# Products without a reader in TensorE's waits, and two key products moved ahead of the second mixture's last second layers

## The chip, the core and the metric

The kernel runs on one core of one Trainium2 chip. The metric is the device time of one execution in microseconds (us); a kernel's time is the median of several executions. TensorE multiplies matrices into PSUM, VectorE (DVE) and ScalarE (ACT) read PSUM and write PSUM or SBUF, GpSimd (POOL) works on SBUF, and SyncE issues the DMAs. The engines run side by side and wait for each other through semaphores. Each engine executes its own instructions in the order in which they are written. TensorE's clock has two levels in the trace, 2.4 GHz (shown as 1.00) and 1.2 GHz (0.50).

## The reference, cut to what matters

Input is x of 8 batches of 128 rows with 128 columns, and a context of the same shape. Four layers follow each other, each made of an attention-like part and a feed-forward part, and both add to x:

```python
x = x + tanh(g_xattn[0]) * mlstm(layernorm(x), ctx, ctx, ...)             # recurrence
x = x + tanh(g_ffn[0])   * pick_one_of_8(layernorm(x), ...)               # first mixture
x = x + tanh(g_xattn[1]) * attention_16_heads(layernorm(x), ctx, ctx)     # first attention
x = x + tanh(g_ffn[1])   * ternary_linear(layernorm(x))                   # rows scaled to 8 bits
x = x + tanh(g_xattn[2]) * attention_mask_group(layernorm(x), ctx, ctx)   # second attention
x = x + tanh(g_ffn[2])   * top_8_of_64_experts(layernorm(x))              # second mixture
x = x + tanh(g_xattn[3]) * attention_relative_bias(layernorm(x), ctx)     # third attention
x = x + tanh(g_ffn[3])   * (shared + top_2_of_8)(layernorm(x))            # third mixture
```

An attention is `softmax(q k^T / sqrt(8) + bias) v` per head, then an output projection. An expert is `silu(x Wg) * (x Wu)` times a weight of its token, then `Wd`.

## The kernel before, in words

The whole of x stays in SBUF. A product of 32-bit precision is made of three 16-bit products, high by high, high by low, low by high (`three` and `products`, L235 and L225), so that one product over half of the tokens is three instructions of 512 columns. Nearly every product is issued at L228.

The three attentions are numbered a = 0, 1, 2. Each has three stretches:

- The head (`head_pe`, `head_act`, `head_dve`): normalisation, the turn of the normalised x by TensorE (L460), and 16 jobs e = 0 to 15 (keys and queries, `proj_pe`), each three products by TensorE, one activation by ScalarE (L1782) and one sum by DVE (L1789). Jobs 0 and 1 of a head are keys, need only the context, and are issued earlier: for a = 2 in `turn_y_pe`, after the second mixture's last second layer and ahead of the turn of its result (L1653).
- The attention itself (`att_pe`): per batch b, scores by rows (`att_rows`, L1893), their maxima by DVE (L1915), the maxima turned (`att_max_pe`; L1950 and L1952 for a = 0, L1948 for the others), scores by columns (`att_cols`, L1984), the exponentials by ScalarE (L2002), their products with the values (`att_pv`, L2021 and L2027), the quotient by DVE (L2035), the output product (`att_out`, L228). For a = 1 there are six small DVE instructions after the maxima (`att_max_split`, L1925 to L1934) and a multiplication by POOL (L2006). The last jobs 13, 14 and 15 of the head stand among the first scores.
- The tail, inside `att_pe`, after the last batch's scores: the last two output products, the residual by DVE (L2072), the normalisation of the last three batches, and their turn (`turn_one_pe`, L481), ScalarE's high part (L485), DVE's low part (L489). For a = 1 and 2 the router of the next mixture follows (`route_pe`, 24 small products; `route_dve`, L936 to L974).

The mixtures run over chunks of 128 hidden units: 48 for the second (`moe1_pe`), 10 for the third (`moe_pe`). Per chunk TensorE makes a gate product, an up product and a second layer (`moe_pe_down`) for each half of the tokens. In the second mixture DVE multiplies gate by up (L1115, raises `w1_gated`), weighs (L1128) and takes the low part (L1264); ScalarE makes SiLU (L1064) and the high part (L1093). At the end ScalarE copies the two halves of the result (L1675), TensorE turns them (L1653), and DVE adds them to x (L1698). The first instructions of the third head's DVE program are these sums.

`fill_pe(pe, at, n)` (L784) issues n products of 128 x 128 by 512 columns of the context into bank `at`; nobody reads the result. The kernel before uses it in the recurrence and in the first mixture only (58 products in all). PSUM has 8 banks of 512 columns; which one a product writes decides whom it must wait for.

## Time and profile before

| | |
|---|---|
| median of 3 runs | 635.67 us (635.35 to 637.15) |
| the profiled execution's own time | 636.67 us |
| its span, first to last instruction | 634.9 us |
| mean granted clock of TensorE | 0.962 |
| busy: TensorE, DVE, ACT, POOL | 562.7, 518.2, 340.1, 249.3 us |
| `fill_pe` products (L787) | 58, 16.5 us busy |

The profiled execution took 1.8 us more than its span. Its mean clock is below 1 because the granted clock goes to 0.50 in eight stretches, 47.8 us in all. The first, at 45.45 to 48.86 us, is at the end of the recurrence. By time the span is: recurrence to about 49 us, first mixture to 120, first attention with its head and tail to 190, second to 284, second mixture to 501, third attention to 582, third mixture to the end.

### The profile page before, as it was taken

To read this page: it belongs to the slowest core of one execution; us is meant where nothing else is said; L and a number is where in the kernel's file an instruction comes from. 1 tells how busy PE (TensorE), PEld (TensorE's weight loads), DVE (VectorE), ACT (ScalarE), POOL (GpSimd) and SP (SyncE) were. 2 spreads that over 40 slices of the span, in tenths; PEclk is the share of its full clock that TensorE was granted. 3 is DMA by queue.
4 is the path that set the end of the run, shared out by engine and by line. 5 is a ranking of instruction groups with operands and counts; after the bars stand their busy time and mean duration, and the time that the engine had idled before them with its cause. 6 is when DMAs were issued, how large, how long until landed. Compare 5 with 4: busy or idle time off the path is not lost.

```text
span 634.9 us, 16313 instructions
## 1 busy us (share of the span) xinstructions
PE 562.7 (89%) x5394; PEld 289.0 (46%) x5394; DVE 518.2 (82%) x1136; ACT 340.1 (54%) x675; POOL 249.3 (39%) x456
## 2 busy tenths in 40 slices
PE   4899899968878799967999999999999779996997
PEld 2444588725644255533444343333433325553443
DVE  6798886877889778848899999999999786766896
ACT  3878776555545333434555565555655463343654
POOL 3475010301772168872344443444334100234452
PEclk9999999987998799979999999999999899997999
DMA  8600200240000000002566656666666000001110
GB/s 316 214 2 2 69 3 2 40 117 2 4 2 0 2 2 3 3 1 69 155 179 176 175 170 162 180 181 169 163 173 182 4 2 2 2 3 31 38 50 33
DMA packets 34912, 48.89 MB, mean 77 GB/s; under 512 B 6756, under 2 KB 26800, under 8 KB 34472
## 3 DMA queue, kind: packets, MB, share of 16 engines
q1 hardware_dynamic: 34424, 47.40, 26.4%
q8 instruction: 37, 0.61, 0.4%
q10 hardware_dynamic: 432, 0.73, 0.3%
q14 instruction: 19, 0.16, 0.1%
HBM read 47.29 MB, written 0.82 MB: 76 GB/s over the span
## 4 chain that ended last, share of the span: by engine, by line
PE 44%; DVE 41%; ACT 6%; issue 4%; POOL 3%; DMA 1%; DVEq 0%; ACTq 0%; POOLq 0%
PE PS L228 29%; DVE PS L1115 9%; DVE SHARED L1264 5%; DVE SHARED L1789 4%; DVE PS L1128 3%; PE PS L2021 2%; ACT SHARED L1093 2%; PE PS L2027 2%; DVE MB L1915 2%; ACT SHARED L1064 2%; PE PS L1893 2%; DVE REC L2035 1%; DVE PS L1915 1%; DVE STAT L394 1%; DVE XN L410 1%
## 5 line engine op out<-in xcount | busy, mean ns | idle before, releaser
L1093 ACT ACTIVATE SHARED<-PS 128x512 f16<-128x512 f32 x96 | 57.1, 597 | 71.8 <-DVE PS L1128 68.2
L228 PE MATMUL PS<-XH,UH 128*128 128x512 f16 x232 | 89.9, 387 | 6.2 <-DVE PS L1115 3.4
L228 PE MATMUL PS<-XL,UH 128*128 128x512 f16 x232 | 89.5, 386 | 0.0
L228 PE MATMUL PS<-XH,UL 128*128 128x512 f16 x232 | 89.4, 385 | 0.0
L2002 ACT ACTIVATE SHARED<-PS 128x512 f32<-128x512 f32 x96 | 52.2, 595 | 64.9 <-PE PS L228 49.7
L228 PE MATMUL PS<-SHARED,DNH 128*128 128x512 f16 x232 | 69.9, 383 | 4.6 <-DVE SHARED L1264 3.7
L1264 DVE TENSOR_TENSOR SHARED<-PS,SHARED 128x512 f16<-128x512 f32 x96 | 62.0, 686 | 6.8 <-ACT SHARED L1093 3.4
L1064 ACT ACTIVATE SHARED<-PS 128x512 f32<-128x512 f32 x96 | 57.2, 597 | 17.4 <-PE PS L228 15.0
L1022 POOL CAST DNH<-DF 128x128 f16<-128x128 f32 x58 | 19.0, 327 | 117.2 <-DMA DF<-in_down 100.7
L1128 DVE TENSOR_TENSOR PS<-PS,SHARED 128x512 f32<-128x512 f32 x92 | 59.7, 694 | 3.8
L1115 DVE TENSOR_TENSOR PS<-SHARED,PS 128x1024 f32<-128x1024 f32 x46 | 56.5, 1229 | 6.7 <-PE PS L228 0.7
L1915 DVE TENSOR_REDUCE MB<-PS 128x4 f16<-128x512 f32 x64 | 41.1, 687 | 16.8 <-PE PS L228 11.0
L2006 POOL TENSOR_TENSOR SHARED<-SHARED,GPT 128x512 f32<-128x512 f32 x32 | 40.0, 1270 | 26.2 <-ACT SHARED L2002 26.1
L1782 ACT ACTIVATE SHARED<-PS,LOB,LOM 128x512 f16<-128x512 f32 x48 | 35.2, 774 | 25.8 <-PE PS L228 25.8
L228 PEld LDWEIGHTS PS<-XH,UH 128*128 128x128 f16 x232 | 22.9, 99 | 50.5 <-DVE PS L1115 25.1
L228 PE MATMUL PS<-SHARED,DNL 128*128 128x512 f16 x116 | 44.5, 384 | 0.0
L1015 POOL TENSOR_TENSOR UL<-UF,UH 128x256 f16<-128x256 f32 x58 | 39.2, 676 | 4.6
L2021 PE MATMUL PS<-SHARED,ONE 128*32 128x128 f32 x768 | 40.7, 285 | 0.0
L2027 PE MATMUL PS<-SHARED,V 128*32 128x128 f32 x768 | 39.4, 278 | 0.6 <-POOL SHARED L2006 0.6
L1789 DVE SCALAR_TENSOR_TENSOR SHARED<-PS,BQK,SHARED 128x512 f16<-128x512 f32 x48 | 33.5, 738 | 6.9 <-ACT SHARED L1782 6.8
L228 PEld LDWEIGHTS PS<-SHARED,DNH 128*128 128x128 f16 x232 | 22.3, 98 | 33.9 <-issue 7.3
L228 PEld LDWEIGHTS PS<-XH,UL 128*128 128x128 f16 x232 | 23.0, 99 | 28.4 <-issue 1.7
(345 smaller groups left out, 1275.5 us busy)
## 6 DMA issues: line engine op xcount, KB each, us to landing
SHARED<-w_rows_dram SPq DMA_DIRECT2D x31, 384.0 KB, 3.6
SHARED<-w_rows_dram SPq DMA_DIRECT2D x30, 256.0 KB, 3.8
UF<-in_up SPq DMA_DIRECT2D x58, 128.0 KB, 3.4
SHARED<-w_rows_dram SPq DMA_DIRECT2D x31, 128.0 KB, 2.7
DF<-in_down SPq DMA_DIRECT2D x58, 64.0 KB, 3.0
V<-in_up SPq DMA_DIRECT2D x2, 1024.0 KB, 9.1
SHARED<-in_down SPq DMA_DIRECT2D x4, 512.0 KB
SHARED<-t_values_dram SPq DMA_DIRECT2D x2, 1024.0 KB, 10.5
```

Source lines behind the costliest of these rows:

```text
L228: last = pe.matmul(dst, l, r, start=start and i == 0, stop=stop and i == len(pairs) - 1)
L1064: act.activation(SG1[u][:, hf, :], bank(hf), ACT.Silu).then_inc(sem("e_act"), 1)
L1093: act.activation(HHI[:, u, hf, :], bank(4 + hf) if m == 1 else HF[:, hf, :], ACT.Copy).then_inc(sem("e_high"), 1)
L1115: dve.tensor_tensor(dst, SG1[u].rearrange("p i n -> p (i n)"), bank(2, 2), ALU.mult).then_inc(sem("w1_gated"), 1)
L1128: dve.tensor_tensor(bank(4 + hf), bank(4 + hf), WB[u][:, HALF * hf:HALF * hf + HALF], ALU.mult)\
L1264: dve.tensor_tensor(HLO[:, u, hf, :], src, HHI[:, u, hf, :], ALU.subtract).then_inc(sem("e_low"), 1)
L1789: dve.scalar_tensor_tensor(dst, proj_bank(a, "kq", e), BQK[:, a, "qk".index(c), g:g + 1], TLO[:, e % 4, :], ALU.add, ALU.subtract).then_in ...
L1915: dve.tensor_reduce(dst, src, AX, ALU.max, negate=True).then_inc(sem("a_max"), 1)
L2002: act.activation(PF[:, j, :], bank(2 + j % 2), ACT.Exp).then_inc(sem("a_exp"), 1)
L2006: pool.tensor_tensor(PG[:, j, :].rearrange("p (g s) -> p g s", g=4), PF[:, j, :].rearrange("p (g s) -> p g s", g=4), over(GPT[:, b, :], 4) ...
L2021: pe.matmul(bank(4 + u)[32 * g:32 * g + 32, 128:256], ONE8[:, j, :], PF[:, j, 128 * g:128 * g + 128], start=j == 0, stop=j == 3, skip_grou ...
L2027: last = pe.matmul(bank(4 + u)[32 * g:32 * g + 32, 0:128], V32[:, b, 4 * g + j, :], src[:, j, 128 * g:128 * g + 128], start=False, stop=j ...
```

## The change

It adds calls of `fill_pe` on TensorE's queue at places of the attentions: around the first batch of the first two attentions (`FILL`, 16 and 13 products), in the second head ahead of and behind the first turn (7 and 2), in the tails of the second and the third attention (`FILL_TAIL` and a last 2: 22 and 18), and at the end of the second mixture (3). These are 81 products. Each group stands directly ahead of an instruction with a wait. It also moves jobs 0 and 1 of the third head: on TensorE from behind the last second layers to ahead of them, with a wait on `w1_gated` for DVE's product of the last chunk, because these jobs write banks 2 and 3, from which that product reads; on ScalarE from behind the two copies of the mixture's result to ahead of them. Since `turn_y_pe` is reached for m = 1 and 2 only, the lines taken out of it were executed for m = 1 alone. No computed value changes.

```diff
--- before.py
+++ after.py
@@ -1241,6 +1241,10 @@
                 step(2 * i + 1, 1, i)
             step(CH2 - 2, 0, CH2 // 2 - 1)
             step(CH2 - 1, 1, CH2 // 2 - 1)
+            pe.wait_ge(sem("w1_gated"), CH2)
+            for e in (0, 1):
+                proj_pe(pe, 2, "k", e)
+            fill_pe(pe, 0, 3)
             for hf in range(2):
                 moe_pe_down(pe, 1, CH2 - 1, 1, hf, stop=True)
             turn_y_pe(pe, 1)
@@ -1644,9 +1648,6 @@
 
         def turn_y_pe(pe, m):
 
-            if m < 2:
-                for e in (0, 1):
-                    proj_pe(pe, 2 * m, "k", e)
             for i in range(2):
                 pe.wait_ge(sem("y_out"), 2 * m - 1 + i)
                 for b in range(4 * i, 4 * i + 4):
@@ -1668,6 +1669,8 @@
                     moe_act_high(act, m, c, u, hf)
             if m == 1:
                 moe1_act(act)
+                for e in (0, 1):
+                    proj_act(act, 2, "k", e)
             else:
                 chunks(act, m, step)
             for i in range(2):
@@ -1802,8 +1805,11 @@
             proj_pe(pe, a, "v", 0)
             if a != 1:
                 proj_pe(pe, a, "v", 1)
+            if a == 1:
+                fill_pe(pe, 0, 7)
             turn_pe(pe, TURN[a], NORM[a], (0,), TURN_AT)
             if a == 1:
+                fill_pe(pe, 5, 2)
                 quant_turn_pe(pe, 1)
                 proj_pe(pe, a, "k", 4)
                 quant_product_pe(pe, 1)
@@ -1821,7 +1827,7 @@
                 proj_pe(pe, a, "kq"[e >= 8], e)
 
         def head_act(act, a):
-            for e in range(4):
+            for e in range(2 if a == 2 else 0, 4):
                 proj_act(act, a, "k", e)
             proj_act(act, a, "v", 0)
             if a != 1:
@@ -2075,6 +2081,9 @@
 
         NEXT = ((3, None), (5, 4), (7, 6))
 
+        FILL = ((6, 0, 3, 3, 4), (2, 7, 0, 0, 4), (0, 0, 0, 0, 0))
+        FILL_TAIL = (None, (2, 6, 3, 2, 7), (3, 2, 3, 2, 6))
+
         def att_pe(pe, a):
             k, j = NEXT[a]
             if a == 2:
@@ -2082,8 +2091,10 @@
                 pe.wait_ge(sem("ld_late"), 16 * len(LATE))
             att_rows(pe, a, 0, 0)
             proj_pe(pe, a, "q", 13)
+            fill_pe(pe, 4, FILL[a][0])
             att_rows(pe, a, 0, 1)
             proj_pe(pe, a, "q", 14)
+            fill_pe(pe, 4, FILL[a][1])
             att_max_pe(pe, a, 0, 0)
             proj_pe(pe, a, "q", 15)
             att_rows(pe, a, 1, 0)
@@ -2092,13 +2103,19 @@
                 u = b % 2
                 if b == 1:
                     pe.wait_ge(sem("p_lo"), 16 * (a + 1))
+                if b == 0:
+                    fill_pe(pe, 4, FILL[a][2])
                 att_cols(pe, a, b, u, 0)
+                if b == 0:
+                    fill_pe(pe, 4, FILL[a][3])
                 if b + 1 < NB:
                     att_rows(pe, a, b + 1, 1)
                 if b >= 1:
                     att_pv(pe, a, b - 1, 1 - u, 2)
                     att_pv(pe, a, b - 1, 1 - u, 3)
                 att_cols(pe, a, b, u, 1)
+                if b == 0:
+                    fill_pe(pe, 4, FILL[a][4])
                 if b + 1 < NB:
                     att_max_pe(pe, a, b + 1, 1 - u)
                 if b >= 2:
@@ -2116,15 +2133,22 @@
             if a == 0:
                 quant_product_pe(pe, 0)
                 proj_pe(pe, 1, "k", 0)
+            if j:
+                fill_pe(pe, 2, FILL_TAIL[a][0])
             att_out(pe, a, NB - 2, 0)
             if a == 0:
                 proj_pe(pe, 1, "k", 1)
             if j:
+                fill_pe(pe, 2, FILL_TAIL[a][1])
                 turn_one_pe(pe, a, j, k, NB - 3)
+                fill_pe(pe, 2, FILL_TAIL[a][2])
             att_out(pe, a, NB - 1, 1)
             if j:
+                fill_pe(pe, 2, FILL_TAIL[a][3])
                 turn_one_pe(pe, a, j, k, NB - 2)
+                fill_pe(pe, 2, FILL_TAIL[a][4])
                 turn_one_pe(pe, a, j, k, NB - 1)
+                fill_pe(pe, 2, 2)
 
         def att_act(act, a):
             k, j = NEXT[a]
```

## Rows read from the trace of the kernel before

**Rows 1.** The page: TensorE's clock in 40 slices, the chain's shares by engine.
```profile
PEclk9999999987998799979999999999999899997999
...
PE 44%; DVE 41%; ACT 6%; issue 4%; POOL 3%; DMA 1%; DVEq 0%; ACTq 0%; POOLq 0%
```

**Rows 2.** Stretches (from:to, length; busy PE, PEld, DVE, ACT, POOL; clock; DMA).
```profile
137.61:141.02 3.41, 3.24 (x11) 1.01 (x9) 2.06 (x4) 0.78 (x1) 0.00 (x0) 0.50 0.00 0
144.43:151.26 6.83, 5.80 (x99) 4.10 (x97) 3.86 (x6) 2.77 (x5) 0.00 (x0) 0.50 0.01 2
195.63:199.05 3.42, 2.75 (x14) 1.55 (x14) 3.38 (x8) 1.97 (x3) 0.00 (x0) 0.50 0.00 0
212.70:219.53 6.83, 5.83 (x33) 2.11 (x35) 3.81 (x9) 1.42 (x3) 0.16 (x1) 0.50 0.02 5
277.55:287.79 10.24, 6.06 (x39) 3.10 (x40) 4.36 (x19) 1.97 (x6) 6.41 (x14) 0.50 0.07 19
496.01:499.42 3.41, 3.02 (x8) 1.12 (x9) 0.83 (x2) 0.98 (x3) 0.00 (x0) 0.50 0.00 0
577.92:588.16 10.24, 7.05 (x41) 2.88 (x41) 6.71 (x44) 3.33 (x7) 4.84 (x12) 0.50 0.17 46
```

**Rows 3.** TensorE in order of time, start of the second attention.
```profile
211.49 0.38 PE L228 MATMUL PS<-XH,WRL 128*128 128x512 f16 x1
213.70 0.61 PE L1948 MATMUL PS<-EYEH,MB 128*128 128x128 f16 x4 [1.83 <-DVE MB L1934]
214.10 0.63 PE L228 MATMUL PS<-XH,WRH 128*128 128x512 f16 x1
214.53 0.64 PE L228 MATMUL PS<-XL,WRH 128*128 128x512 f16 x1
...
222.85 0.40 PE L1948 MATMUL PS<-EYEH,MB 128*128 128x128 f16 x4 [1.19 <-DVE MB L1934]
```

**Rows 4.** TensorE and DVE in order of time, start of the first attention.
```profile
137.13 0.40 PE L1893 MATMUL PS<-SHARED 24*128 24x128 f16 x8 [1.78 <-DVE MB L1915]
...
147.47 1.30 DVE L1915 TENSOR_REDUCE MB<-PS 128x4 f16<-128x512 f32 x2 [1.66 <-PE PS L1893]
...
151.64 0.96 DVE L2035 RECIPROCAL REC<-PS 128x128 f32<-128x128 f32 x1 [0.35 <-PE PS L2027]
```

**Rows 5.** The second head: a wait of TensorE, and a stretch as in rows 2.
```profile
194.55 1.09 PE L460 MATMUL PS<-EYE,XN 128*128 128x128 f32 x4 [2.05 <-DVE XN L410]
...
193.00:206.00 13.00, 10.78 (x60) 5.46 (x60) 12.96 (x37) 7.23 (x12) 2.10 (x3) 0.87 0.00 0
```

**Rows 6.** The chain that ended last (start, us, what), second attention's tail and router.
```profile
279.12 0.84 PE PS L228 x5
...
282.78 0.49 PE PS L481
...
283.95 1.48 PE PS L228 x24
```

**Rows 7.** In order of time: the end of the second mixture.
```profile
492.93 1.23 DVE L1115 TENSOR_TENSOR PS<-SHARED,PS 128x1024 f32<-128x1024 f32 x1
...
494.93 1.19 ACT L1093 ACTIVATE SHARED<-PS 128x512 f16<-128x512 f32 x2 [2.85 <-DVE PS L1128]
...
496.40 1.01 PE L228 MATMUL PS<-SHARED,DNH 128*128 128x512 f16 x2 [2.59 <-DVE SHARED L1264]
...
500.01 1.45 ACT L1782 ACTIVATE SHARED<-PS,LOB,LOM 128x512 f16<-128x512 f32 x2 [0.26 <-PE PS L228]
...
501.10 0.75 DVE L1698 SCALAR_TENSOR_TENSOR X<-PS,G,X 128x512 f32<-128x512 f32 x1 [4.25 <-PE PS L1653]
```

**Rows 8.** In order of time, then a stretch: third attention's tail, third mixture.
```profile
581.34 0.47 PE L481 MATMUL PS<-EYE,XN 128*128 128x128 f32 x1 [1.39 <-DVE XN L410]
...
588.08 0.22 DVE L974 TENSOR_TENSOR CW<-SHARED,CW 128x64 f16<-128x64 f32 x1
...
589.00:625.00 36.00, 36.00 (x168) 16.23 (x167) 32.36 (x50) 21.25 (x36) 19.90 (x31) 1.00 0.15 39
```

## The prediction

> **What bounds the kernel now.** I read the slices of the page first. TensorE's clock is full in most of them and lower in eight or nine, and the chain that ended last is shared almost evenly by TensorE and DVE [rows 1]. So no engine bounds the whole; each stage has to be read by itself. Then I read the stretches of low clock [rows 2]: seven, at half clock throughout, 3.41 us or two or three times that long, 44.4 us together. All lie where this change works: the start of the first attention (two), the second head, the start of the second attention, the second attention's tail, the end of the second mixture, the third attention's tail. Last I read TensorE in order of time ahead of each. It had waited for DVE shortly before: 1.78 us at 137.13 [rows 4], 2.05 us at 194.55 [rows 5]; the 1.83 us ahead of 213.70 [rows 3] and the 2.59 us ahead of 496.40 [rows 7] lie across the fall itself. The cause of a fall is thus little work for TensorE, and its price is paid by whatever TensorE does next. A low stretch costs something only where TensorE, not DVE, is late in it.
>
> **The price of a product.** At full clock 168 products, nearly all of 512 columns, fill 36.00 us [rows 8], 0.22 us each; at low clock two such start 0.43 us apart (214.10 and 214.53) [rows 3]. A reader-less product therefore costs 0.22 us of TensorE's queue, and nothing of the time if it fits the wait behind it. The groups against their waits: 6 products, 1.3 us, before the wait of 1.78 [rows 4]; 7, 1.5 us, before 2.05 [rows 5]; 7, 1.5 us, before 1.83, and 4, 0.9 us, before 1.19 [rows 3]; 3, 0.7 us, before 2.59, with the two key jobs (six products, 1.3 us) ahead of them [rows 7]; 6, 1.3 us, before 1.39 [rows 8]. Each fits at full clock, the last one barely, so I cost the 81 products at nothing. If none were hidden they would cost 81 x 0.22 = 17.8 us; that is the bound on the other side. They read the context and write a bank that is free at that place, and no other engine waits for them.
>
> **First attention's start: 3.0 us gained.** With 1.3 us of products in the wait before 137.13, and 10 more in the waits of the first batch, the clock has no reason to fall at 137.61 or at 144.43. What was slow between 137.61 and 151.26 was partly TensorE: DVE was busy only 2.06 of 3.41 and 3.86 of 6.83 us there [rows 2]. I follow the chain. Jobs 14 and 15 and the turned maxima end 1.1 us earlier (nine products of 512 columns or their like, half of it behind DVE). The second batch's scores and the first batch's eight groups of value products, then at half price, end 1.9 us earlier; DVE's waits such as the 1.66 us before 147.47 go. The first reciprocal, at 151.64 [rows 4], comes at about 148.6. Behind it DVE sets the pace and the shift stays.
>
> **Second head: nothing.** DVE was busy 12.96 of the 13.00 us around the low stretch [rows 5]. TensorE's slower products there were covered by DVE. Its clock rises, the time does not.
>
> **Second attention's start: 2.0 us.** Between 212.70 and 219.53 TensorE was busy 5.83 of 6.83 us and DVE 3.81 [rows 2]. Job 15, sixteen small products and nine of 512 columns stand between 213.70 and 219.4. At full clock they need about 3 us instead of 5.7. Some 0.7 us of this go to DVE's own work (job 15's sum and the maxima follow each other), so the turn at 222.85 [rows 3] comes about 2.0 us earlier.
>
> **Second attention's tail and router: 1.2 us.** The chain runs through TensorE four times: turns of 0.49 us twice (the second at 282.78), an output product of 0.84, 24 router products of 1.48 [rows 6]. At full clock I take 0.14 off each turn, 0.28 off the output product and 0.6 off the router (24 x 0.025). The rest of the tail is a relay of ACT, DVE and POOL, whose steps no clock changes. The 22 products lie in its gaps. Bounds: 0 if the clock falls all the same, 1.3.
>
> **End of the second mixture: 2.2 us.** Here the order is what counts. TensorE stood for 2.59 us before the last second layers (496.40), which wait for DVE's low parts, then made these six products and the two key jobs at low clock, and only then the turns that DVE's sum at 501.10 waits for [rows 7]. After the change the key jobs run in the wait. They need `w1_gated` of the last chunk, DVE's product at 492.93, which ends at 494.2 [rows 7]; with three fillers they end at 496.1, ahead of the second layers' own release, just under 496.4. Behind this new wait stand only instructions that waited anyway. ScalarE now makes the two key activations (1.45 us, before at 500.01) ahead of the copies of the result; it is free for them from 496.1, when the last high parts end [rows 7], so the copies, which I take at 0.6 us, start at about 497.6. The turns no longer stand behind the key jobs, the first half is copied at 498.2 and turned at 498.8, and DVE's sum comes at 498.9 instead of 501.10. DVE sets the pace of the head that follows, so 2.2 us stay; 1.5 of them would come from order alone with the clock up in both kernels. POOL and SyncE have no step in this; the queues' DMAs are unchanged.
>
> **Third attention's tail and router: 0.3 us.** Two turns and an output product, 0.3 us at full clock. The rest of the low stretch, the third mixture's first twelve products (5.2 us at low clock, 2.6 at full), stands beside the router's DVE chain, which ends at 588.08 [rows 8] and on which TensorE's next turn waits. So these 2.6 us are not gained.
>
> **What it may trigger.** They come back as an idle stretch instead. At full clock TensorE ends the twelve products at about 585.5 and waits until 587.8, 2.3 us or more, as long as the waits ahead of the falls above. I expect a fall there; it would reach into the third mixture, where TensorE is busy 36.00 of 36.00 us [rows 8]. The shortest stretch of rows 2, 3.41 us, then costs half of itself, 1.7 us. The same can happen in the second mixture's first 10 us, where the router's chain is DVE's too; half of such a stretch would meet TensorE's own path.
>
> **The sum.** Against the profiled execution, 636.67: less 3.0 + 2.0 + 1.2 + 2.2 + 0.3 = 8.7, plus 1.7 for one new low stretch in a mixture, gives 629.7. The median of the three runs is 1.0 us below the profiled one. I don't take this off: the runs differ by where their low stretches lie, I suppose, and the change removes most of these.
>
> The Trainium skill ("TensorE: Matmul & The Clock Gate", section "What's actually happening") says that the penalty of the slow ramp is below 1% of a typical kernel's span and that the count of slow products differs from run to run. That speaks against a gain above 6.3 us: by it the time would be 630.3 or more. Here the trace has 44.4 us at half clock in the places named, 7% of the span [rows 2], so I go by the rows; the forecast needs nothing of the page.
>
> **Rivals.** (a) As summed, one new fall: 629.7, chance 0.45. (b) No new fall: the idle stretch before 587.8 is short enough, or its place relative to the clock's decision is lucky: 628.0, chance 0.30. For it: there are waits of more than 1 us that no fall follows, such as the one before 222.85 [rows 3]. (c) New falls in both mixtures, each 1.7: 631.4, chance 0.12. For it: both routers are the same kind of DVE chain. (d) The products don't hold the clock, the low stretches stay, and only the moved key jobs pay: 636.67 - 2.2 = 634.5, chance 0.08. Against it: the stretches in front of the falls are nearly idle, and the change fills half or more of each. (e) Slower: the clock is already low when TensorE reaches the fillers. Then each costs 0.43 us, and the waits are too short. The three groups of 6, 7 and 7 at the starts and the head would be late by 0.8, 1.0 and 1.2 us and the 6 of the last tail by 1.2, together 4.2 us for 26 products; 81 at that rate give 13, less 2.2 for the order: 647. It decides from the point where a group is longer than its wait: at low clock 4 products fill 1.78 us. Chance 0.05. Against it: rows 3 show full clock up to 211.49, directly ahead of a group.
>
> **How the numbers follow.** The likeliest case is (a). From 0.2 under (b)'s time less the 1.0 us of the unprofiled runs, to (c) plus 1.2, the range is 626.8 to 632.6; outside lie (d), (e) and tails of (b) and (c), about 2 in 10. A difference of 0.3%, 1.9 us, is about what a measurement of this kernel can tell from no change. Faster by more than that: (a), (b), (c), 0.87. Within: (d), 0.08. Slower: (e), 0.05.
>
> **What would show it.** In the changed kernel's trace the clock should be 1.00 from 130 to 200 us and again in the second attention's start; the reciprocal that was at 151.64 should be at about 148.6, the turn at 222.85 about 5.0 earlier, the router of the second mixture 6.2 earlier, the sum at 501.10 8.4 earlier, and a low stretch should appear at the third mixture's beginning. The waits of TensorE in front of which fillers stand should have shrunk, not vanished; one that is gone, with DVE or ACT waiting behind it, is a filler that delays. The prediction is wrong if the second head gains, if the shift of one attention's start is lost before its tail (then POOL, not DVE, sets the pace there), or if low stretches stay where the fillers are.

## The result, and the profile after

| | before | after |
|---|---|---|
| median, from lowest to highest (20 executions each, on the same chip) | 637.44 us (633.83 to 640.27) | 634.79 us (630.25 to 637.13) |
| profiled execution | 636.67 us | 634.09 us |
| its span | 634.9 us | 632.3 us |
| mean granted clock of TensorE | 0.962 | 0.989 |
| low clock within the span | 47.8 us in eight stretches | 13.7 us in three stretches |

The ratio of after to before is 0.995, with a 95% interval of 0.9932 to 0.9968: faster, by 2.65 us where 7.0 were forecast against the profiled execution. 629.7 was predicted, with a range of 626.8 to 632.6, and 634.79 lies outside it.

One part of the gap between the medians is in no profile. The 20 executions of the changed kernel took 1.7 to 1.8 us more than their spans. Those of the kernel before, in the runs made beside the experiments, took 1.7 to 3.1 us more, with medians of 2.1 to 2.8. No run here settles why.

The page of the changed kernel, where [rows 1] stood before: the slices of TensorE's clock and the shares of the chain that ended last.

```profile
PEclk9999999999999999997999999999999899999999
DVE 43%; PE 40%; ACT 7%; issue 4%; POOL 3%; DMA 1%; DVEq 0%; ACTq 0%; POOLq 0%
```

The clock is held nearly everywhere now. Next, the changed kernel by stretches, with the busy time and count of TensorE, its weight loads, DVE, ACT and POOL, then the granted clock, the DMA share and GB/s. The first two lines cover the starts of both attentions; the other five are the three low stretches and what stands directly ahead of two of them.

```profile
130.00:200.00 70.00, 58.87 (x983) 34.68 (x984) 60.49 (x139) 38.02 (x71) 31.61 (x56) 1.00 0.07 18
205.00:280.00 75.00, 70.10 (x1012) 36.63 (x1012) 54.55 (x150) 28.13 (x60) 50.84 (x61) 1.00 0.01 2
284.10:290.93 6.83, 3.44 (x16) 1.79 (x17) 4.96 (x9) 3.65 (x7) 1.32 (x3) 1.00 0.01 2
290.93:297.76 6.83, 6.83 (x15) 1.97 (x13) 3.90 (x5) 1.79 (x3) 1.06 (x2) 0.50 0.73 199
502.55:505.97 3.42, 3.42 (x12) 1.71 (x11) 3.42 (x9) 2.15 (x3) 0.00 (x0) 0.50 0.01 2
581.06:584.47 3.41, 0.43 (x7) 0.34 (x7) 3.10 (x11) 1.36 (x3) 1.07 (x2) 1.00 0.23 67
584.47:587.89 3.42, 3.42 (x14) 1.44 (x11) 2.19 (x5) 2.55 (x4) 0.00 (x0) 0.50 0.00 0
```

The seven stretches of [rows 2] are gone, and the one at the recurrence's end with them. Three new ones are there: 290.93 to 297.76 in the second mixture's first chunks, 502.55 to 505.97 in the third head, and 584.47 to 587.89 in the third mixture. In the first and the third TensorE is busy all the time and DVE is not (3.90 of 6.83, 2.19 of 3.42 us): there TensorE is late, and the low clock costs time. In the second DVE is busy 3.42 of 3.42 us, and it costs nothing: in the table below the changed kernel gains 0.2 us from 501.10 to 583.35, as routers_filled does, which has no such stretch.

**Where the time went.** DVE executes the same instructions in both kernels, so each can be paired with itself. A shift is its start in one kernel less its start in the profile of before, in us. These are pairs of single profiled executions, good for saying where time moved; how much a kernel gains is read from its ratio. The other kernels are those of the next section.

| DVE instruction, place (start before) | after | routers_filled | tails_empty | order_alone | tails_alone |
|---|---|---|---|---|---|
| first reciprocal, first attention (151.64) | -2.68 | -1.98 | -2.73 | +0.25 | -0.41 |
| last job of the second head (207.10) | -2.66 | -1.96 | -2.17 | +0.27 | +0.66 |
| last small instruction of the maxima, second attention (222.57) | -4.48 | -3.79 | -4.00 | -1.56 | -1.10 |
| reciprocal ahead of its tail (275.69) | -4.44 | -3.75 | -3.98 | -1.53 | -1.07 |
| second router's first (285.45) | -5.58 | -4.89 | -3.98 | -1.70 | -2.21 |
| weighing in the second mixture's first chunk (296.82) | -5.50 | -4.89 | -3.66 | -1.17 | -1.26 |
| the same in its next chunk (301.43) | -2.25 | -4.89 | -3.66 | +1.75 | +1.12 |
| last gated product (492.93) | -2.18 | -4.88 | -3.62 | +1.87 | +1.19 |
| first sum into x (501.10) | -4.58 | -7.28 | -6.02 | -0.52 | +1.40 |
| third router's first (583.35) | -4.77 | -7.47 | -6.02 | -0.32 | +1.22 |
| third router's last (588.08) | -4.23 | -6.93 | -5.38 | -0.30 | +1.76 |
| SiLU product in the third mixture (600.15) | -2.57 | -6.93 | -5.38 | -0.29 | +3.42 |

Rows of the changed kernel from which seven of the first column's entries come: start, duration, engine, line, operation. The lines of the changed kernel that are quoted here stand up to six lower than in the kernel before (L2041 is L2035 there).

```profile
148.97 0.95 DVE L2041 RECIPROCAL REC<-PS 128x128 f32<-128x128 f32 x1
279.87 0.69 DVE L936 COPY SHARED<-PS 128x512 f32<-128x512 f32 x1 [0.97 <-PE PS L228]
291.32 0.70 DVE L1123 TENSOR_TENSOR PS<-SHARED,PS 128x512 f32<-128x512 f32 x1 [2.02 <-PE PS L1212]
299.18 0.70 DVE L1123 TENSOR_TENSOR PS<-SHARED,PS 128x512 f32<-128x512 f32 x1 [2.27 <-PE PS L1212]
...
496.52 0.75 DVE L1701 SCALAR_TENSOR_TENSOR X<-PS,G,X 128x512 f32<-128x512 f32 x1 [1.85 <-PE PS L1654]
...
583.85 0.23 DVE L974 TENSOR_TENSOR CW<-SHARED,CW 128x64 f16<-128x64 f32 x1
...
597.58 0.69 DVE L1102 TENSOR_TENSOR SHARED<-SHARED,PS 128x512 f32<-128x512 f32 x1
```

So the change gains 2.7 + 1.8 + 1.1 + 2.4 + 0.2 = 8.2 us in five places and gives 5.5 back in three: 3.3 between 296.82 and 301.43, 0.5 inside the third router, 1.7 behind it. That leaves 2.7, against the 2.6 between the two profiled executions.

**Two of the five gains are not shown to be the products'.** They are measured against one execution that was at low clock at 212.70 and at 496.01 [rows 2]. order_alone and tails_alone have no product at the second attention's start, and gain 1.8 us there all the same (+0.27 to -1.56, +0.66 to -1.10), because their executions did not fall there. starts_alone (shifts -2.93 at 492.93 and -4.41 at 501.10) has the old order and no product at the end of the second mixture, and gains 1.5 us there at full clock. The first line is order_alone's, the second starts_alone's:

```profile
212.70:219.53 6.83, 4.86 (x50) 2.10 (x51) 4.87 (x13) 2.11 (x4) 2.01 (x2) 1.00 0.02 5
489.00:499.00 10.00, 6.99 (x46) 3.95 (x47) 6.96 (x17) 5.20 (x9) 0.56 (x2) 1.00 0.03 9
```

The other two larger gains do hang on the products. At the first attention's start the two kernels without them are within 0.4 us of before (+0.25, -0.41). In the second attention's tail, from 275.69 to 285.45, tails_alone gains 1.1 us as the changed kernel does, and tails_empty nothing.

**Why the clock falls at the second mixture's start.** TensorE of the changed kernel in order of time, the idle time before an instruction in brackets.

```profile
285.15 0.38 PE L228 MATMUL PS<-XH,UH 128*128 128x512 f16 x1 [2.27 <-ACT SHARED L1064]
...
288.23 1.06 PE L1255 MATMUL PS<-EYE,SHARED 128*64 128x128 f32 x8 [1.62 <-DVE SHARED L953]
...
290.01 2.91 PE L1212 MATMUL PS<-SHARED,SELF 64*128 64x512 f32 x4 [0.72 <-ACT SHARED L1262]
...
293.26 0.63 PE L228 MATMUL PS<-XL,UH 128*128 128x512 f16 x1
```

Three waits, 2.27 + 1.62 + 0.72 = 4.6 us, stand close together ahead of the fall at 290.93. The first is for ScalarE's SiLU, the second for the router's DVE chain. The kernel before has the same three, of 1.49, 1.62 and 0.72 us, and its profiled execution did not fall there, so the change made only the first longer, by 0.8 us. The third mixture's start has one long wait for the router's chain, 2.98 us. The kernel before had none there, because TensorE at low clock was busy until the chain had ended. First two rows of the changed kernel, then one of before:

```profile
584.13 0.76 PE L902 MATMUL PS<-EYEH,CW 128*128 128x128 f16 x8 [2.98 <-DVE CW L974]
584.69 0.63 PE L228 MATMUL PS<-XH,UH 128*128 128x512 f16 x1
```

```profile
588.37 0.62 PE L902 MATMUL PS<-EYEH,CW 128*128 128x128 f16 x8
```

### The profile page after: what moved, and what is told of

It is laid out like the page before. It is cut to its first block, busy times and chain, and to the rows that moved or that the text cites. A ratio compares the mean times of both kernels' runs of the same rounds, so it can differ in the third digit from the quotient of the medians.

```text
span 632.3 us, 16475 instructions
## 1 busy us (share of the span) xinstructions
PE 572.3 (91%) x5475; PEld 291.5 (46%) x5475; DVE 519.3 (82%) x1136; ACT 340.0 (54%) x675; POOL 248.7 (39%) x456
## 4 chain that ended last, share of the span: by engine, by line
DVE 43%; PE 40%; ACT 7%; issue 4%; POOL 3%; DMA 1%; DVEq 0%; ACTq 0%; POOLq 0%
PE PS L228 28%; DVE PS L1115 9%; DVE SHARED L1268 5%; DVE SHARED L1792 4%; DVE PS L1128 3%; ACT SHARED L1093 2%; DVE MB L1921 2%; PE PS L2027 2%; ACT SHARED L1064 2%; PE PS L1899 2%; PE PS L2033 2%; DVE PS L1921 2%; DVE STAT L394 1%; DVE XN L410 1%; DVE REC L2041 1%
## 5 line engine op out<-in xcount | busy, mean ns | idle before, releaser
L1785 ACT ACTIVATE SHARED<-PS,LOB,LOM 128x512 f16<-128x512 f32 x48 | 35.3, 774 | 23.3 <-PE PS L228 23.3
L1015 POOL TENSOR_TENSOR UL<-UF,UH 128x256 f16<-128x256 f32 x58 | 38.8, 669 | 4.6
L787 PE MATMUL PS<-CHI 128*128 128x512 f16 x139 | 36.4, 380 | 0.0
```

## The experiments

Twelve kernels ran, in three groups; the kernels of one group share a chip and the runs of the kernel before. Only fill_between, the last, has runs of its own of the kernel before. Each ratio is against these runs. Their medians lie between 636.29 and 638.74 us, so across groups ratios are compared, and within a group the kernels' own times as well.

**First group: the change taken apart, and its repair.**

The repair, routers_filled, is the changed kernel with 29 more reader-less products in the waits of both routers:

```diff
                 moe1_pe_up(pe, c, u)
+                if static and c == 0:
+                    fill_pe(pe, 4, 9)
...
                 if static and c == 0:
+                    fill_pe(pe, 4, 6)
                     moe1_rows_pe(pe)
+                    fill_pe(pe, 6, 2)
...
                 if isinstance(c, int) and c == 0:
+                    fill_pe(pe, 4, 12)
                     route_turn_pe(pe, 2)
```

> The changed kernel plus 29 reader-less products in TensorE's waits beside the routers: 9 and 6 of them around the second chunk's gate product of the second mixture, 2 ahead of its first weights' products, 12 ahead of the turn of the third mixture's router. Theory 1, the gain is given back by new falls of the clock at the starts of both mixtures: the low stretches at 291 to 298 us and at 584 to 588 us go, 3.3 and 1.3 to 1.7 us come back, and the median is about 5 us below the changed kernel's 634.8, near 630 (ratio to the kernel before 0.988). Theory 2, the shift is lost at the mixtures for another reason (weights that arrive when they arrive, DVE): the median stays at 634.8 or rises with the added products, and the shift against the kernel before shrinks at 293 to 301 us as it did.

Measured: 629.87 us (628.86 to 630.34), ratio 0.9863 [0.9828, 0.9899]. Its profile, by stretch, then its TensorE at the two routers:

```profile
190.00:600.00 410.00, 388.03 (x3164) 178.87 (x3164) 342.65 (x659) 205.79 (x364) 167.71 (x313) 1.00 0.33 87
```

```profile
283.41 2.11 PE L787 MATMUL PS<-CHI 128*128 128x512 f16 x9
...
285.84 0.38 PE L228 MATMUL PS<-XH,UH 128*128 128x512 f16 x1 [0.33 <-ACT SHARED L1064]
...
578.29 2.75 PE L787 MATMUL PS<-CHI 128*128 128x512 f16 x12
581.43 0.62 PE L902 MATMUL PS<-EYEH,CW 128*128 128x128 f16 x8 [0.39 <-DVE CW L974]
581.89 0.38 PE L228 MATMUL PS<-XH,UH 128*128 128x512 f16 x1
```

The clock is full from 190 to 600 us; two low stretches are left ahead of that, at 124.52 and 179.13. The wait of 2.27 us has become nine products and 0.33, the wait of 2.98 has become twelve and 0.39; neither router is later for it. The table of shifts shows both losses gone: 3.3 us at the second mixture's start and 1.7 behind the third router are exactly what the two low stretches had cost. The 0.5 us inside the third router stays.

order_alone is the kernel before with the two key jobs moved, on TensorE as below and on ScalarE as in the change, and no product added:

```diff
+            pe.wait_ge(sem("w1_gated"), CH2)
+            for e in (0, 1):
+                proj_pe(pe, 2, "k", e)
             for hf in range(2):
                 moe_pe_down(pe, 1, CH2 - 1, 1, hf, stop=True)
```

> The kernel before with the two key jobs of the third head moved ahead of the second mixture's last second layers, on TensorE and ScalarE, and no added reader-less product. If order is what pays there, as predicted: 1.5 us from order alone where the clock is up, 2.2 us with it, so DVE's first sum of the third head comes 1.5 to 2.2 us earlier against its neighbours and the median is about 2 us below the kernel before (ratio 0.997). Rival: the order only pays together with the clock that the three products hold up; then 0 to 0.7 us.

Measured: 635.87 us (634.12 to 636.98), ratio 0.996 [0.9935, 0.9986]. From 492.93 to 501.10 its shift goes from +1.87 to -0.52, a gain of 2.4 us. The changed kernel gains the same 2.4 there, so its three products at that place add nothing. Of the 2.4, 1.5 come to starts_alone by the clock alone, in the old order; the new order itself is worth the 0.9 that are left, by the difference of two single pairs. In the profile a low stretch at the second mixture's start hides all of it, which this execution had and the profiled one of before had not:

```profile
294.58:301.40 6.82, 6.82 (x14) 2.08 (x13) 3.90 (x5) 1.27 (x3) 1.07 (x2) 0.50 0.74 196
```

It costs 3.4 us (-1.70 at 285.45 to +1.75 at 301.43) in a kernel in which that place is as it was before. So this fall is not the products' alone: the kernel before can meet it too, and its profiled execution had been spared it.

tails_empty is the changed kernel without the 40 products of the two tails:

```diff
-        FILL_TAIL = (None, (2, 6, 3, 2, 7), (3, 2, 3, 2, 6))
+        FILL_TAIL = (None, (0, 0, 0, 0, 0), (0, 0, 0, 0, 0))
...
-                fill_pe(pe, 2, 2)
```

> The changed kernel without the 40 reader-less products in the tails of the second and the third attention. Theory 1, a low stretch in a tail is cheap because the routers' DVE chain covers the products behind it, and holding the clock there only moves the fall into the mixtures: the tails run at low clock as before (1.1 and 0.3 us lost), the mixtures start at full clock (3.3 and 1.7 us gained back), and the median is 2 to 3.6 us below the changed kernel's 634.8, near 632. Theory 2, the tails' products pay as intended: the median is 1.4 us above the changed kernel's, near 636.

Measured: 631.33 us (630.97 to 632.38), ratio 0.9891 [0.9855, 0.9926]. It is faster than the whole change, with more low clock. The interval lies apart from the change's [0.9932, 0.9968]; it overlaps a little with that of changed_again below, whose 12 executions have a median of 633.79 us. Its stretches:

```profile
272.77:283.01 10.24, 5.25 (x37) 2.84 (x38) 4.37 (x19) 2.51 (x7) 6.41 (x14) 0.50 0.08 19
291.00:298.00 7.00, 6.27 (x22) 2.43 (x20) 4.35 (x7) 3.27 (x6) 1.06 (x2) 1.00 0.49 135
573.14:579.97 6.83, 4.40 (x33) 2.04 (x34) 4.16 (x33) 1.89 (x4) 4.12 (x10) 0.50 0.21 60
```

17 us at half clock in the tails cost 1.1 + 0.2 us, because TensorE is busy about half of them and the relay of ACT, DVE and POOL sets the pace. But with the tails at low clock both mixtures start at full clock. Guarding a cheap place had moved the fall to a dear one. Of the four profiles in which neither the tails nor the second router are guarded (before, order_alone, tails_empty, starts_alone) one fell at the second mixture's start; of the five with the tails guarded and that router not, all did.

starts_alone is the kernel before with the 29 products at the two attentions' starts (`FILL` as in the change, nothing else).

> The kernel before with the 29 reader-less products at the starts of the first two attentions alone. By the predicted sum 3.0 + 2.0 us are gained there (in the changed kernel's profile 2.7 and 1.0 to 1.6 were), the tails run at low clock as before, and nothing else moves: the median is 4 to 5 us below the kernel before (ratio 0.993). Rival: with the starts at full clock other stretches fall in their place, in the second head for one, and the ratio is above 0.997.

Measured: 632.9 us (632.04 to 633.24), ratio 0.9911 [0.9875, 0.9946]. Its shift is -2.16 at the first reciprocal, -3.07 at 222.57, and stays near -3 to 492.93. A low stretch in the second head, 192.23 to 199.06, costs 0.9 of that (shift -2.16 to -1.31). These 29 products alone do at least as well as the whole change (the intervals overlap by little). Of its -3.8 us at the end of the profile, two terms, 1.8 and 1.5 us, are those that are not shown to be the products' (above).

**Second group: single parts, and the tails.**

head_empty is the changed kernel without `fill_pe(pe, 0, 7)` and `fill_pe(pe, 5, 2)` in the second head.

> The changed kernel without the 7 and 2 reader-less products in the second head. DVE covers TensorE there, so a low stretch in the head costs 0 to 0.3 us: DVE's instructions behind the head keep their shift against the kernel before, about -2.7 us up to 213 us, and the median is that of the changed kernel, 634.8, within the noise. Rival: the head's products pay, and the shift at 213 us shrinks by 1 us or more.

Measured: 635.57 us (630.48 to 636.98), ratio 0.9942 [0.9911, 0.9974], not to be told from the change by the median. In the profile a low stretch came back; its line among the stretches, then one row of DVE:

```profile
192.23:199.06 6.83, 6.31 (x23) 2.97 (x24) 6.80 (x23) 2.97 (x5) 0.23 (x1) 0.50 0.00 0
```

```profile
203.09 1.42 DVE L1792 SCALAR_TENSOR_TENSOR SHARED<-PS,BQK,SHARED 128x512 f16<-128x512 f32 x2 [0.82 <-ACT SHARED L1785]
```

DVE is busy 6.80 of 6.83 us in it, as in [rows 5], and yet the shift goes from -2.74 to -1.42. Some 0.35 of that is lost ahead of the head, at a low stretch of this execution in the first attention's tail (178.58 to 181.99). The rest, 1.0, comes in one step: the jobs that TensorE and ACT made late are missed by DVE only after the stretch, at 203.09. The nine products are worth 1.0 us in this profile, where the stretch is twice as long as the one of before.

third_router is the changed kernel with the 12 products ahead of the third router's turn, and nothing at the second.

> The changed kernel plus the 12 reader-less products ahead of the turn of the third mixture's router, and none in the second mixture. If each new fall has its own price: no low stretch at 584 us, the shift at the end of the span keeps what it had at 583 us (1.3 to 1.7 us more than in the changed kernel), the second mixture's start still loses up to 3.3 us in most executions; the median is near 633.3. Rival: the gain of the two fillings together came from the second mixture alone; then the median stays at 634.8.

Measured: 634.53 us (630.19 to 634.98), ratio 0.9933 [0.9904, 0.9963]. The third mixture starts at full clock and keeps its shift, -2.20 from 588.08 to the end. The gain is not seen in the time, because the second mixture fell for longer:

```profile
285.92:299.58 13.66, 12.28 (x29) 4.52 (x27) 7.48 (x12) 4.11 (x7) 1.07 (x2) 0.50 0.42 118
```

That stretch cost 4.9 us (shift -5.20 at 285.45, -0.31 at 301.43). The same place cost 3.3 to 3.4 in every profile with a stretch of 6.8 us there (after, changed_again, head_empty, tails_alone, order_alone), half of its length. What an unguarded wait costs goes by the length of the stretch, and that differs between executions of nearly the same kernel.

routers_no_tails is routers_filled without the tails' 40 products (the edit of tails_empty).

> The changed kernel with the 29 products beside the routers and without the 40 in the tails. Theory 1: with the mixtures' starts guarded the tails' products keep what they gain there, 1.2 + 0.3 us, so this kernel is about 1.5 us slower than the one with both, 631.4 against 629.9. Theory 2: the tails' products gain nothing even then, and this kernel is equal or faster, 629.9 or less.

Measured: 631.91 us (631.81 to 633.35), ratio 0.9898 [0.9861, 0.9935]. Against routers_filled in profile it is 0.8 us behind after the second tail (-4.09 against -4.89 at 285.45), 1.2 at 501.10, 1.5 at 588.08 and 2.2 at 600.15 (-4.76 against -6.93). The last 0.7 are not the tails' own. With the tails at low clock TensorE reaches the 12 products of the third router later, and they end behind the router's chain (the turn L902 waits for nothing):

```profile
581.02 2.75 PE L787 MATMUL PS<-CHI 128*128 128x512 f16 x12
583.61 0.61 PE L902 MATMUL PS<-EYEH,CW 128*128 128x128 f16 x8
```

So the same 40 products that make the changed kernel slower (0.995 with them, 0.9891 without, the intervals apart) are worth about 2 us once the routers are guarded. And the routers' 29 without the tails' 40 bring nothing over tails_empty (631.91 against 631.33 us). They pay only together.

tails_doubled is routers_filled with every group of the tails at twice its size (`FILL_TAIL` (4, 12, 6, 4, 14) and (6, 4, 6, 4, 12), and 4 for the last 2).

> The kernel with the 29 products beside the routers, and every group in the two tails doubled (4, 12, 6, 4, 14, 4 and 6, 4, 6, 4, 12, 4 products). The groups are then longer than their waits, by 0.2 to 1.3 us each at 0.22 us a product: about 2.5 us late in the second attention's tail, about 2.9 us in the third's, so 5 us above the 629.9 of the kernel with single groups, near 635. If the waits absorb them or the engines behind cover them, it stays under 632; a price of 0.22 us for all 40 added products would give 638.7.

Measured: 633.9 us (633.35 to 634.92), ratio 0.9931 [0.9904, 0.9959]. In profile it is 4.1 us behind routers_filled, with a mean clock of 0.997. Up to the second tail it was 0.75 us ahead (-4.50 against -3.75 at 275.69), so the doubling costs 4.8: 3.0 in the second tail, 1.5 in the third, 0.4 between them. Twelve products fill 2.75 us, so the 40 more are 40 x 0.22 = 8.8 us, of which 4.8 came through and the rest still fitted the waits. The forecast of 5 had the right size: a group that outgrows its wait delays at once, at full clock too.

**Third group: repeated, turned around, and extended.**

changed_again is the changed kernel once more.

> The changed kernel itself, on the chip of the two others, to tell how far its profile varies. By theory 1 its executions differ by which stretches fall: the shift against the kernel before is -8 us less what the falls at the mixtures' starts take, 0 to 5.5 us, and the executions with the higher mean clock are the faster ones, at about 1 us for a low stretch of 3.41 us (0.0027 of mean clock). Median near 634.8.

Measured: 633.79 us (630.49 to 635.56), ratio 0.9932 [0.9904, 0.996]. The same two falls are in its profile, in other places by 0.4 us:

```profile
291.30:298.13 6.83, 6.83 (x15) 1.89 (x13) 3.90 (x5) 1.79 (x3) 1.06 (x2) 0.50 0.79 212
584.85:588.26 3.41, 3.41 (x12) 1.22 (x9) 2.27 (x5) 2.55 (x4) 0.00 (x0) 0.50 0.00 0
```

Over its 12 executions and the 20 of the first measurement, time and granted clock go together (correlation -0.89). The three shortest of the 20, 630.25 to 630.62, have clocks of 0.992 to 0.997; the five longest, 636.17 to 637.13, have 0.978 to 0.981. The mean clock is not all: at 0.992 changed_again has executions of 630.6 and of 634.37 us, the second of them the profiled one with both falls in the mixtures. Where the low stretches lie counts too.

tails_alone is the kernel before with the tails' 40 products alone.

> The kernel before with the 40 reader-less products in the tails alone. Theory 1: 1.1 and 0.3 us are gained in the tails, and new low stretches at the starts of the second and the third mixture take up to 3.3 and 1.7 us, so the kernel is 0 to 3 us slower than the kernel before (ratio 1.000 to 1.005). Theory 2, the tails pay by themselves: 1.4 us faster (ratio 0.998).

Measured: 639.91 us (633.16 to 641.02), ratio 1.0015 [0.998, 1.005]. The two stretches in the profile, which stood in neither mixture before:

```profile
293.40:300.23 6.83, 6.83 (x12) 2.35 (x13) 2.97 (x5) 1.19 (x2) 0.19 (x1) 0.50 0.62 172
590.36:593.78 3.42, 3.42 (x15) 1.50 (x13) 2.10 (x4) 2.54 (x4) 0.00 (x0) 0.50 0.00 0
```

They cost 3.3 us (-2.21 at 285.45 to +1.12) and 1.7 (+1.76 to +3.42). The median lies 3.6 us above that of before in this group, while the ratio's interval has 1 in it. Half of the change by count of its products brings no measurable gain and moves the low clock from the tails, where it costs 1.3, into the mixtures, where it costs 5.0 in this profile. The 12 executions lie in two clusters, five at 633.2 to 635.3 and seven at 639.7 to 641.0 us; the profiled one, 640.12, is of the upper. That the lower five were spared the falls is likely, but no trace of one shows it.

fuller is routers_filled with 17 more products in the remaining waits of the third attention's start and of the two ends of the first attention.

> The kernel with the 29 products beside the routers and 17 more: 2 and 4 in the first attention's tail, 5 ahead of the third attention's first scores, 6 in its first batch. In the profile of the kernel without these a low stretch at 179 to 182.5 us took about 1 us. If the products hold the clock there as elsewhere and are hidden, the median is about 1 us lower, 629, and the executions lie closer together; if they are late at the tail's short waits (0.9 and 0.5 us), it is 0.2 to 1 us higher.

Measured: 629.35 us (629.08 to 630.13), ratio 0.9887 [0.9857, 0.9916]. It can't be told from routers_filled: the intervals overlap, and they ran in different groups. In its profiled execution the stretch in the first attention's tail is still there, at 179.17 to 182.59, though six of the 17 products stand there; in three of the other five the mean clock is 1.000. Whether the last waits are worth guarding stays open.

fill_between is routers_filled with the 12 products of the third router one step earlier, between the up products of the first chunk's two halves:

```diff
                 for hf in range(2):
+                    if isinstance(c, int) and c == 0 and hf == 1:
+                        fill_pe(pe, 4, 12)
                     moe_pe_up(pe, m, c, u, h, hf)
                 if isinstance(c, int) and c == 0:
-                    fill_pe(pe, 4, 12)
                     route_turn_pe(pe, 2)
```

> The kernel with the 29 products beside the routers, its 12 products of the third mixture placed between the first chunk's first and second half of the tokens instead of behind both. In the changed kernel DVE's L967 took 0.72 us where it took 0.23 before, while POOL's UL<-UF,UH (L1015), released by TensorE's last up product, ran at the same time. If that is one disturbing the other, the later up product lets POOL run behind the router's DVE chain, L967 takes 0.23 us again, the third mixture's second chunk starts 0.5 us earlier, and the profile's shift at the end is about 0.5 us more; the median is 0.3 to 0.5 us below 629.9. Rival: L967 is slow for another reason (ScalarE's SiLU, TensorE at full clock); it stays at 0.72 us and the median at 629.9 or above, because ScalarE's second SiLU comes later.

Measured: 628.99 us (628.45 to 629.68), ratio 0.9863 [0.9822, 0.9903]. The 0.5 us inside the router are back. First the changed kernel, then fill_between: DVE's chain and POOL's instruction beside it.

```profile
581.83 0.67 POOL L1015 TENSOR_TENSOR UL<-UF,UH 128x256 f16<-128x256 f32 x1
581.86 0.72 DVE L967 TENSOR_TENSOR SHARED<-SHARED 128x64 f32<-128x64 f32 x1
```

```profile
579.18 0.22 DVE L967 TENSOR_TENSOR SHARED<-SHARED 128x64 f32<-128x64 f32 x1
...
580.68 0.23 DVE L974 TENSOR_TENSOR CW<-SHARED,CW 128x64 f16<-128x64 f32 x1
...
581.87 0.67 POOL L1015 TENSOR_TENSOR UL<-UF,UH 128x256 f16<-128x256 f32 x1
```

POOL's instruction and the one ahead of it follow TensorE's up products of the first chunk, whose weights they replace. At full clock these end early enough for L1015 to meet L967 (in the kernel before it ran at 589.05, behind the chain); with the fillers between them they end later, and it starts when the chain is done. ScalarE's SiLU is ruled out as the cause: in fill_between it ran at 578.80 for 0.60 us, beside L966 and L967, and they took 0.22 us each. In tails_empty, starts_alone and routers_no_tails the same POOL instruction comes later in the chain and meets its last steps, at a price of 0.6 us. These are tails_empty's rows:

```profile
581.95 0.67 POOL L1015 TENSOR_TENSOR UL<-UF,UH 128x256 f16<-128x256 f32 x1
581.98 0.68 DVE L973 CAST CW<-SHARED 128x64 f16<-128x64 f32 x1
```

L973 took 0.19 us in the kernel before. This is the shortest median of all, and its lead over the changed kernel is shown by the ratios of both against the kernel before; its lead over routers_filled, 0.5 us, is shown in the profile only.

## Why the prediction was wrong, step by step

**Right in the numbers, in part by luck.** The places of the five gains held. The five gains were forecast as 3.0, 2.0, 1.2, 2.2 and 0.3 us, together 8.7; they measured 2.7, 1.8, 1.1, 2.4 and 0.2, together 8.2. The first and the third are shown to be the products'. The second and 1.5 us of the fourth came to kernels without products in those places too: there the sum was right because the execution that it started from had fallen, and a run of before that is spared has nothing to gain. The clock is 1.00 from 130 to 200 us and through the second attention. The waits shrank and did not vanish, such as these of the changed kernel's second tail, where [rows 6] stood:

```profile
274.54 0.23 PE L228 MATMUL PS<-WH,ATH 128*128 128x128 f16 x1 [0.24 <-DVE ATL L2060]
...
277.94 0.33 PE L481 MATMUL PS<-EYE,XN 128*128 128x128 f32 x1 [0.49 <-ACT XN L781]
```

At the end of the second mixture the order forecast from [rows 7] came about. ACT makes the key activations (L1785) ahead of the copies (L1678), and DVE's sum, quoted above at 496.52, is no longer behind the key jobs:

```profile
493.84 1.44 ACT L1785 ACTIVATE SHARED<-PS,LOB,LOM 128x512 f16<-128x512 f32 x2
495.17 1.14 ACT L1678 ACTIVATE SHARED<-PS 128x512 f32<-128x512 f32 x2
```

Only the split was off: 1.5 of the 2.2 us were put down to the order with the clock up in both kernels, where order_alone against starts_alone, both at full clock there, shows 0.9.

**Wrong: "What it may trigger", and with it the last term of the sum, plus 1.7.** This term measured 5.5, in three parts.

1. The second mixture. The text allowed a fall there, at the price of half of a stretch of 3.41 us, left it out of the sum and put it into rival (c) with a chance of 0.12. It came in every profile in which the tails were guarded and the second router was not: after, changed_again, head_empty, third_router and tails_alone; and in order_alone's, whose tails are not guarded. It lasted 6.8 or 13.7 us, not 3.41, and cost 3.3 to 4.9 us (3.3 in the changed kernel), not 1.7. The shortest stretch of [rows 2] was taken for the price, where four of the seven are two or three times as long. And the reason that the text gave for the third mixture, that a faster TensorE waits longer for a chain that no clock shortens, holds for the second router as much; only the chance was set lower.
2. The third mixture. This fall was forecast, at the right place and price: 1.7 us, and a wait of 2.98 where "2.3 us or more" was written.
3. The third router, 0.5 us: L966 and L967 beside POOL. No step of the prediction had it: POOL is not in what it says of the third tail and router.

By these numbers the sum reads 636.67 - 8.2 + 5.5 = 634.0, and 634.09 was measured. Rival (c), falls in both mixtures, was the case that came, at 631.4 by its prices; with 3.3 and 1.7 for its two falls and 0.5 for the contention it would have read 633.5. That the range ended at 632.6 follows from the same undersized price and the missing contention. (b), no fall, may be what the shortest executions of the changed kernel come near to (630.25 at clock 0.997, forecast 628.0); no trace of one shows where its clock was low. routers_filled has no fall in the mixtures, at 629.87. (d) and (e) did not come: the products held the clock where they stand.

**Wrong in part: "second head: nothing".** That reading holds for the profile of before, in which DVE covered the low stretch. It does not hold for head_empty and starts_alone, where a stretch twice as long cost 1.0 and 0.9 us. That DVE is busy through a low stretch shows only that it has work in hand; the lateness can be met behind it.

**The base.** The sum was made against one execution of before that had full clock at both mixtures' starts. The kernel before lies between 633.83 and 640.27; order_alone shows that the mixtures' starts can fall without the change. So part of the 5.5 us is not new in kind, as part of the 8.2 us is not the change's, and the ratio of 0.995, or 2.65 us between the medians, is the fair statement of what the change gives.

**The skill's rule.** The text cited the Trainium skill ("TensorE: Matmul & The Clock Gate", section "What's actually happening"): penalty of the slow ramp below 1% of a typical kernel's span, count of slow products different from run to run; by an estimate from it 630.3 or more. The time did come out above 630.3, though because the clock fell elsewhere. routers_filled, whose clock is held from 190 to 600 us, is 1.4% faster than the kernel before; order_alone is 0.4% faster, and the 1% that is left lies at the edge of what the rule allows. Its second half agrees with the trace: between executions of one kernel the clock differs, 0.978 to 0.997, and the time with it.

## What to carry to other kernels

Guarding a wait can move a low stretch rather than remove it: the sum must ask at each later place where TensorE waits for a chain of another engine, whether a fall there meets TensorE's own path, and take as its bound a stretch as long as the longest that the trace shows, not the shortest. So guard all long waits up to the next dense stretch, or leave the cheap places at low clock and let the clock be up again in time (tails_empty, 0.9891, beats the change, 0.995; all guarded, 0.9863, beats both). Fit each group of products into its wait at 0.22 us a product, since twice the size cost 4 us in the time; and where executions of a kernel spread over 1%, forecast from what can fall, not only from what fell in the one profile, and profile the kernel before more than once, since a place that fell by chance looks like a gain in whatever is compared with it.

## What the runs showed of the hardware

**DVE beside POOL.** A DVE addition of 128x64 with both inputs in SBUF (L967) took 0.22 us alone and 0.72 us while POOL's 128x256 instruction of 0.67 us ran, and it started 0.03 us behind it. The Trainium skill ("SBUF — State Buffer", section "Who interferes with whom") states that a DVE instruction with two SBUF inputs contends with a GpSimd instruction that reads SBUF. The trace agrees, with 0.5 us more for L967 and 0.13 more for L966, which ran beside POOL's cast L1013 (0.35 instead of 0.22). The cast L973 has one SBUF input, and took 0.68 instead of 0.19 us beside the same POOL instruction in tails_empty. What was not expected is who brought it about: a faster TensorE released POOL earlier, into DVE's chain.

**A low stretch costs half its length where TensorE is the late engine.** 6.8 us at half clock cost 3.3 to 3.4 us in five profiles at the second mixture's start, and 3.4 us cost 1.3 to 1.7 in four at the third's; 10.24 us in the second tail cost 1.1.

**A low stretch need not follow one long wait.** At 290.93 it followed waits of 2.27, 1.62 and 0.72 us with work between them (TensorE busy 3.44 of the 6.83 us ahead), at 584.47 one wait of 2.98 (busy 0.43 of the 3.41 us ahead). Nor does a fall follow such a group always: the kernel before had 1.49, 1.62 and 0.72 us at the first place and kept the full clock in its profiled execution. Why the first lasted 6.83 and the second 3.42 us, and why the stretch in third_router lasted 13.66, no run here settles.
